# The logarithm's part of delta joins the projection in PSUM through TensorE instead of VectorE

## What is computed

```python
def _L0_attn_ref(x, x_proj_w, dt_proj_w, dt_proj_b, A_log, D_param):
    x_dbl = jnp.einsum('bld,kd->blk', x, x_proj_w)
    delta_un = x_dbl[..., :dt_rank]
    Bm = x_dbl[..., dt_rank:dt_rank + d_state]
    Cm = x_dbl[..., dt_rank + d_state:]
    delta = jax.nn.softplus(jnp.einsum('blr,dr->bld', delta_un, dt_proj_w) + dt_proj_b)
    A = -jnp.exp(A_log)
    delta_a_exp = jnp.exp(jnp.einsum('bld,dn->bldn', delta, A))
    delta_b_x = jnp.einsum('bld,bln,bld->bldn', delta, Bm, x)
    ...
    def step(state, inp):
        dae, dbx, c = inp
        state = dae * state + dbx
        y = jnp.einsum('bdn,bn->bd', state, c)
        return (state, y)
    ...
    return y + x * D_param

xn = _layernorm(x, axis=-1)
s = _L0_attn_ref(xn, ...)
g = _silu(_L0_ffn_ref(xn, ...))
x = x + s * g
```

## Time and profile before

| | us |
|---|---|
| median of 3 executions | 2138.73 |
| lowest, highest | 2136.42, 2140.28 |
| the profiled execution | 2138.38 |
| its span in the trace | 2136.4 |
| first batch starts its scans | 45.5 |
| a batch between | 127.9 to 131.8 |

### The profile page before, as it was taken

The page is one execution under the profiler, slowest core; times in us unless marked ns, Lnnn a source line. Parts: engine busy times, 40 slices in busy tenths (PEclk is TensorE's granted clock), DMA queues, the critical chain, the costliest instruction groups (busy, mean ns, idle before and its releaser), DMA issues.

```text
span 2136.4 us, 30310 instructions
## 1 busy us (share of the span) xinstructions
PE 1831.2 (86%) x8688; PEld 1197.2 (56%) x8688; DVE 1912.2 (90%) x2740; ACT 1491.5 (70%) x2850; POOL 1866.4 (87%) x1004
## 2 busy tenths in 40 slices
PE   4498998989889898997989889898898989989895
PEld 2265655656556565655656556565565656556554
DVE  4577899898989989899898999989899898999997
ACT  3556768686686867768676686866868677686764
POOL 2768999898998989999898998989899899998996
PEclk8698998999999899999999999899999999999997
DMA  6769889898897989989898897989889898898995
GB/s 217 289 205 348 291 290 353 258 366 261 319 317 258 373 251 353 294 275 363 257 349 256 316 330 255 379 254 340 304 273 362 257 364 266 310 334 259 395 302 153
DMA packets 279350, 640.76 MB, mean 300 GB/s; under 512 B 22272, under 2 KB 22784, under 8 KB 268944
## 3 DMA queue, kind: packets, MB, share of 16 engines
q1 hardware_dynamic: 185776, 446.36, 59.6%
q10 hardware_dynamic: 68832, 125.34, 16.2%
q0 software_dynamic: 24576, 67.13, 11.4%
HBM read 516.58 MB, written 122.16 MB: 299 GB/s over the span
## 4 chain that ended last, share of the span: by engine, by line
PE 33%; DVE 26%; issue 16%; DMA 11%; ACT 8%; POOL 5%; SPq 3%; DVEq 0%; ACTq 0%; POOLq 0%
PE z_ps L1186 17%; DVE scan_ps L1033 10%; DMA xo<-in_x 6%; DVE p_sb L1043 6%; DVE h_sb L1033 5%; PE proj_ps L1136 4%; PE y_ps L1202 4%; POOL dbx L521 2%; ACT scan_ps L731 2%; PE y_ps L1219 2%; PE xt_ps L1171 2%; SPq L361 2%; DMA xn<-in_x 1%; PE proj_ps L1128 1%; ACT r_sb L752 1%
## 5 line engine op out<-in xcount | busy, mean ns | idle before, releaser
L521 POOL TENSOR_TENSOR dbx<-b_sb,u_sb 128x1024 f32<-128x1024 f32 x512 | 1233.4, 2502 | 125.5 <-DVE h_sb L1033 65.1
L1033 DVE TENSOR_TENSOR_SCAN scan_ps<-scan_ps,dbx 128x512 f32<-128x512 f32 x704 | 851.1, 1218 | 117.0 <-ACT scan_ps L731 104.3
L731 ACT ACTIVATE scan_ps<-delta,a_sb 128x512 f32<-128x512 f32 x1024 | 701.6, 688 | 350.4 <-DVE p_sb L1043 319.8
L1186 PE MATMUL z_ps<-w_sb,xsT 128*128 128x512 f32 x1920 | 896.8, 611 | 43.0 <-ACT r_sb L752 41.9
L1186 PEld LDWEIGHTS z_ps<-w_sb,xsT 128*128 128x128 f32 x1920 | 358.2, 197 | 418.5 <-issue 415.0
L1202 PE MATMUL y_ps<-ident,p_sb 128*128 128x128 f32 x2816 | 437.8, 287 | 174.2 <-DVE p_sb L1043 164.9
L1202 PEld LDWEIGHTS y_ps<-ident,p_sb 128*128 128x128 f32 x2816 | 341.0, 147 | 330.6 <-DVE p_sb L1043 221.7
L1043 DVE TENSOR_TENSOR p_sb<-scan_ps,c_sb 128x512 f32<-128x512 f32 x704 | 473.0, 672 | 6.5 <-PE y_ps L1202 6.5
L532 POOL TENSOR_TENSOR pp_sb<-h_sb,c_sb 128x1024 f32<-128x1024 f32 (+1 forms) x192 | 394.5, 2054 | 65.1 <-PE y_ps L1219 51.7
L1033 DVE TENSOR_TENSOR_SCAN h_sb<-scan_ps,dbx 128x512 f32<-128x512 f32 x320 | 388.0, 1213 | 16.9 <-ACT scan_ps L731 16.3
L1188 PE MATMUL z_ps<-eb_sb,expert_hot 128*128 128x512 f32 x240 | 190.9, 796 | 0.0
(11 more groups left out here) (128 smaller groups left out, 1419.4 us busy)
## 6 DMA issues: line engine op xcount, KB each, us to landing
w_sb<-in_ew SPq DMA_DIRECT2D x240, 1024.0 KB
b_sb<-bc_rows SPq DMA_DIRECT2D x64, 1024.0 KB, 11.5
ys_rows<-r_sb ACTq DMA_DIRECT2D x240, 256.0 KB
xs<-xs_rows ACTq DMA_DIRECT2D x238, 256.0 KB
c_sb<-bc_rows SPq DMA_DIRECT2D x64, 512.0 KB, 12.4
xn<-in_x SPq DMA_DIRECT2D x16, 1024.0 KB, 15.7
c_sb<-bc_rows SPq DMA_DIRECT2D x16, 1024.0 KB, 13.1
xo<-in_x SPq DMA_DIRECT2D x64, 256.0 KB
```

The lines of the kernel that those rows point to most:

```text
L521: nc.gpsimd.tensor_tensor(dbx[:, k % DBX_PAIRS], b_sb[:, 2 * m:2 * m + 2, :], u_sb[:, dt % 2, :].unsqueeze(1).to_broadcast([P, 2, T]), ALU ...
L731: nc.scalar.activation(scan_ps[:, bank_of(j), :], delta[:, dt % 2, :], ACT.Exp, scale=a_sb[:, dt, n:n + 1]).then_inc(da_ready, 1)
L1033: nc.vector.tensor_tensor_scan(state, bank, dbx[:, j // 2 % DBX_PAIRS, r % 2, :], 0.0, ALU.mult, ALU.add).then_inc(scanned, 1)
L1186: nc.tensor.matmul(z_ps[:], xsT[:, slot, c, :], w_sb[:, i % WRING, c, :], start=(c == 0), stop=False)
```

## The change

The addition in `delta_u` (L933) is taken out. In its place PE multiplies the unit matrix by `u_sb`, which holds the logarithm, and accumulates onto the bank (`add_log`). It waits for ACT's logarithm and maximum, and DVE's multiplication waits for it through `d_sum`. `add_log` stands one unit after `COPY_AT`, ahead of all else that PE has at that unit, and the multiplication now stands two units after `COPY_AT`. NK, NR, NS and NZ0 with their copies, `rank` and the keeping of delta are set later by one to three units. The placing of expert tiles is as before.

```diff
 STEPS = {0: "Z1", 9: "Z2", 16: "NT0", 18: "NT1", 20: "NT2", 23: "NT3", 25: "NX0", 27: "NX1", 30: "Z3",
-         37: "NK", 41: "NR", 43: "NS", 46: "NZ0"}
+         40: "NK", 43: "NR", 45: "NS", 48: "NZ0"}
...
 COPY_AT = {6: "Z1", 15: "Z2", 22: "NT0", 24: "NT1", 25: "NT2", 28: "NT3", 31: "NX0", 34: "NX1", 37: "Z3",
-           46: "NR", 48: "NS", 51: "NZ0"}
+           48: "NR", 50: "NS", 53: "NZ0"}
...
-DELTA_AT = {10: "Z1", 19: "Z2", 41: "Z3", 55: "NZ0"}
+DELTA_AT = {11: "Z1", 20: "Z2", 42: "Z3", 58: "NZ0"}
...
-         "apply": (16, 17, 18, 18), "gate": 34, "rank": 40}
+         "apply": (16, 17, 18, 18), "gate": 34, "rank": 42}
...
             def delta_u(b, par, dt):
                 k = b * DT + dt
-                dve.wait_ge(sp_ready, k + 1)
-                dve.wait_ge(sp_max, k + 1)
-                nc.vector.tensor_tensor(proj_ps[:], proj_ps[:], u_sb[:, dt % 2, :], ALU.add).then_inc(d_sum, 1)
                 dve.wait_ge(d_sum, k + 1)
...
-                    name = copies.get(j - 1)
+                    name = copies.get(j - 2)
                     if name and name[0] == "Z":
                         delta_u(b, par, int(name[1]))
...
+            def add_log(b, dt):
+
+                k = b * DT + dt
+                pe.wait_ge(sp_ready, k + 1)
+                pe.wait_ge(sp_max, k + 1)
+                nc.tensor.matmul(proj_ps[:], ident[:], u_sb[:, dt % 2, :], start=False, stop=True,
+                                 skip_group_check=True).then_inc(d_sum, 1)
...
                 for j in range(UNITS):
+                    name = copies_at(b).get(j - 1)
+                    if name and name[0] == "Z":
+                        add_log(b, int(name[1]))
+                    elif name == "NZ0" and not is_last(b):
+                        add_log(b + 1, 0)
                     name = steps.get(j)
```

## The result

The changed kernel takes 2260.02 us (median; 2256.1 to 2264.75) where the kernel before, measured beside it, takes 2139.51 us: a ratio of 1.0565, 95% interval 1.054 to 1.0591, slower by 120.5 us. The forecast was 2230 us, slower by 92; the direction and the place of the main loss were right. One term of the sum was much too small, and a second one somewhat, so that the time lies above the forecast's own range of 2210 to 2250 us and inside the wide one of 2185 to 2268 us.

What follows compares the result with a forecast made beforehand. ACT and PE each bound a stretch of the batch, DVE paced the rest. Terms 0 + 2.75 + 2.8 + 0.6 = 6.15 us a batch, 94 us in total, gave 2230 us; own range 2210 to 2250, wide range 2185 to 2268.

Steps and rivals of the forecast that it cites:

- Z1: Addition at unit 7: PE's matmul fits its idle time, no wait to speak of; 0 us, bounds -0.7 and +0.3.
- Z2: Addition at unit 16: PE's matmul stands behind the tile of unit 15, DVE waits 3.2 us; +2.75 us a batch.
- Z3: Addition at unit 38: behind the tile of unit 36 and two products, DVE waits 4.4 us; +2.8 us a batch.
- NZ0: Addition at unit 54: DVE waits 1.3 us, less 0.7 removed; +0.6 us a batch, bounds -0.7 and +2.1.
- the 1.5: Between the product of unit 42 and tile of unit 44, PE was to gain 1.5 us on DVE.
- the 0.7 removed: Each addition taken from DVE was to save 0.7 us, 2.8 us a batch, where DVE sets the pace.
- The moved steps: NR, NS and the B and C copy come two units later, then `bc_rows`' DMA; costed 0, up to 3 us.
- POOL and the DMAs: Later `rank` holds POOL's scatters back about 3 us; taken as 0, 1 us kept. DMA behind SP's wait costed 0.
- First and last batch: Z2 and Z3 stand in both; estimated at 3 us for the first batch and 5 us for the last.
- The clock: Rival: one tile a batch in PE's own stretch takes 5.51 instead of 3.67 us; +28 us, 2258 us; chance 0.22.
- Absorbed: Rival: the `xo` wait shrinks by 1.4 us and NZ0's 1.3 us wait goes; about 2192 us; chance 0.19.
- Faster: Rival: DVE is the bound, PE's sums arrive in time, 43.5 us fall off the path; 2095 us; chance 0.05.

Runs made afterwards that it cites:

- experiment 12: Changed kernel with `rank` at unit 43 instead of 42, behind the product of unit 42; 2259.38 us, ratio 1.0566.
- experiment 5: Changed kernel with NZ0's projection on PE at unit 47 instead of 48, ahead of that unit's expert tile; 2255.53 us, ratio 1.0562.
- experiment 6: Kernel of experiment 4 with NZ0's projection at unit 47 instead of 48; 2144.84 us, ratio 1.0036.
- experiment 10: Kernel of experiment 4 with NK, NR, NS and NZ0 one unit earlier, `rank` at 41, delta of Z3 kept at 41; 2163.24 us, ratio 1.0136.
- Experiment 1: Changed kernel with the addition given back to DVE, just before the multiplication, all moved steps kept; 2157.05 us, ratio 1.0093.
- experiment 8: Changed kernel with ACT's softplus of NZ0 at unit 54 instead of 53, multiplication at 56, delta kept at 59; 2250.03 us, ratio 1.0536.
- experiment 11: Changed kernel with the expert tile of unit 47 cut to one of its four products in batches 1 to 14; 2243.69 us, ratio 1.0481.
- experiment 4: Changed kernel with PE's additions of Z2 and Z3 ahead of the expert tiles of units 15 and 36; 2148.94 us, ratio 1.0058.
- Experiment 9: Kernel of experiment 4 with ACT's softplus of NZ0 one unit later; 2137.58 us, ratio 1.0003.
- experiment 7: Addition on PE ahead of the tiles of units 15, 36 and 51, with the step tables of the kernel before; 2143.53 us, ratio 1.0026.

## Why the prediction was right, and where not

- **Z1, 0: right, with no margin.** In batches 1 to 14 there is no wait for the sum. But the matmul stands at half clock in 13 of them and takes 1.9 us and more, not 1.16, and ends 0.04 to 0.1 us before the multiplication starts. Units 0 to 15 became 0.56 us shorter, inside the stated bounds.
- **Z2, +2.75: right in mechanism, too small by 0.65.** Five of 14 batches wait 2.96 us, where 3.2 was forecast; the matmul took 1.02 us there and not 1.16. The other nine wait 3.80 us. In those nine the tile of unit 11 takes 5.4 us instead of 3.7 (640.17 above), which delays the tile of unit 15 and with it the addition. In the kernel before, no tile of unit 11 is slow. The mean wait is 3.50; the rest of the +3.40 is a scan at unit 17 that waits some 0.4 us for its exponential.
- **Z3, +2.8: right.** The wait is 4.22 us in every batch from 1 to 14 (forecast 4.4), `rank` no longer waits (forecast), and the stretch is +2.70.
- **NZ0, +0.6: wrong, +2.26.** The working had PE 2.8 us late and then took 1.5 us off, because PE was said to gain on DVE between the product of unit 42 and the tile of unit 44. That step failed. It compared 2.2 us with the 3.7 of the earlier trace rows, and those 3.7 are of a batch at half clock: in nine of the 14 batches before, that distance is 2.30 us. Rows of the kernel before, one batch on, product of unit 42 and tile of unit 44:

```profile
806.06 0.67 DVE L1043 TENSOR_TENSOR p_sb<-scan_ps,c_sb 128x512 f32<-128x512 f32 x1
...
809.02 3.60 PE L1186 MATMUL z_ps<-w_sb,xsT 128*128 128x512 f32 x8
```

  It is 2.29 us in nine batches of the changed kernel too, so there was nothing to gain, and experiment 12 shows that a gain at unit 44 is lost again by unit 47, because PE has to wait for DVE's products in between. PE's lateness is made behind the product of unit 46. From that row (859.44 in the changed kernel) PE works without a wait up to the end of the addition at 874.02, 14.6 us, and DVE without its two waits would be at the multiplication 12.0 us after it. Without the 1.5 the working gives 2.8 us of wait; the changed kernel and experiments 5, 6, 10 and 12 show 2.5 to 2.65 at full clock, wherever it falls. Less the 0.7 removed that is +1.9, and half clock adds to it: in five of the 14 batches the wait at unit 53 is 2.4 to 3.65 us instead of 2.07.
- **The moved steps, 0: wrong in its reason, hidden in its size.** The working asked what stands behind NR, NS and the copies on SP and POOL, and not who stands behind NZ0's projection. That projection moved behind the tile of unit 47, and ACT, in order, holds the exponential of unit 53 behind the softplus that waits for it. Experiment 1 prices the moves at 20 us without any addition on PE. In the changed kernel this wait and the one at NZ0 add up to the same 2.6 us of lateness, 0.76 of it ACT's own work, which is why removing either alone brought nothing (experiment 5) or a part (8, 11).
- **POOL and the DMAs.** POOL waits 94.8 us in all for the row numbers (L543 above), in the middle of each batch, and DVE does not feel it: its lead over DVE is 0.57 us at unit 52, just enough. With `rank` one unit later it is not (experiment 12). I kept 1 us for it and took 0; 0 was right by a narrow margin.
- **First and last batch**, +3 and +5: measured +1.3 and +8.4. The last batch has its tiles at other units, one of them at unit 5, ahead of Z1's addition, so that DVE waits at Z1 there too, by the row below; the forecast counted Z2 and Z3 only.

```profile
2135.72 0.69 DVE L933 TENSOR_TENSOR u_sb<-proj_ps,xT 128x512 f32<-128x512 f32 x1 [3.45 <-PE proj_ps L1167]
```

- **The rivals.** *The clock*: its 2258 us is nearest to the 2260 measured, but not by its mechanism. A slow tile a batch in PE's own stretch did not come; the granted clock of units 21 to 37 is 1.00 in all of batches 1 to 14, as before. But nine slow tiles came just ahead of it, at unit 11, each of which made the wait at Z2 0.85 us longer, some 8 us of its 28. *Absorbed*: the wait for `xo` fell from 18.0 to 8.5 us over the run, 0.7 a batch, half of the 1.4 assumed, and part of this came back as waits for ACT (0.39 us at unit 8, where there was none). The wait at NZ0 did fall from 2.8 to 0.57, only to appear at unit 53. *Faster*: excluded, as its own condition said. The Trainium skill ("Perfetto Trace Analysis", Identifying the Most-Contended Engine) would relieve the busiest engine first. This was done, DVE's busy time fell from 1912 to 1877 us and its share from 90% to 83%, and the time rose by 5.65%. Even with the sum in time at Z2 and Z3 the relief is worth 8 us (experiments 1 and 4). What decides is which engine's instruction ends last at a place, and at Z1 that is ACT, in units 21 to 37 PE.

That the time stayed within the range, with one term 1.7 us a batch too small and one 0.65, is partly luck: units 0 to 15 gave 0.56 back, and Z1's matmul ended just in time at half clock.

**What stays open.** No version beat the kernel before. Experiment 9 matches it. Whether a placing exists that keeps `rank` free of its wait, PE's addition ahead of the tile of unit 51 and POOL in time was not settled. Also open is why experiment 7's units 16 to 29 take 27.56 us, the same as before, though an addition is gone from them; by the scans' waits it is ACT, at units 17 (0.47 us, none before) and 25 (1.99, 1.85 before). And why the tile of unit 11 became slow in some batches and not in others is not shown.

## What to carry to other kernels

When work goes from one in-order engine to another, do not ask what it costs there but what stands before it: a matmul of 1 us behind a tile of 3.7 us cost some 4 us a batch at each of two places, and ahead of the tile nothing. For every step that is moved, look at who reads it and what is queued behind that reader. And before a distance is used from one batch, look whether the other batches have it: here the batch that was read was one of five whose clock had fallen, and nine had not.

## What the runs showed of the hardware

In the kernel before, the tile of unit 8, behind PE's idle time, is slow in all 14 batches (4.5 to 6.1 us where others take 3.6 to 3.7), and no tile of unit 11 is. With the addition of DVE given back (experiment 1) it is the same. In the changed kernel, with the addition on PE in that idle time, the tile of unit 8 takes 3.6 to 3.9 us in 11 of 14 batches, and the tile of unit 11, behind a wait of about 2 us for ACT, takes 5.4 in nine. So in this kernel a matmul of 1.9 us at half clock, put into a gap, came with a fast tile behind that gap and, in most batches, a slow one behind the next. That is no rule: in experiment 12, whose PE order is that of the changed kernel, the tile of unit 8 is slow in six batches and that of unit 11 in none, and in the other runs with the addition on PE the tile of unit 11 is slow in five to nine. The windows from 640.0 to 646.0 us (tile of unit 11) and from 713.0 to 722.0 us (from the wait for the product of unit 42 on) show it in the granted clock (columns as in the earlier trace rows):

```profile
640.00:646.00 6.00, 5.83 (x13) 2.75 (x14) 5.79 (x8) 6.00 (x14) 5.83 (x4) 0.72 0.65 238
713.00:722.00 9.00, 8.04 (x29) 6.09 (x29) 8.86 (x12) 4.90 (x8) 8.24 (x6) 0.65 0.63 229
```

0.72 and 0.65 are means of stretches with both levels, 1.2 and 2.4 GHz. Gaps of the same kind ended differently from batch to batch: after the wait of 3.4 us for the product of unit 42 PE went on at full clock in nine batches and at half clock in five.
